# Attention loop with three score banks, maxima in a ring of three banks, and one group of projection products per unit

## The chip, the cores and the metric

The kernel runs on one core of one Trainium2 chip. The metric is the device time of one execution, in microseconds (us).

## The reference

An attention block and a sparse feed-forward, each followed by a residual add and a layer norm, in float32. x has 4 batches of 512 rows of 512 columns.

```python
q = (x @ wq).reshape(bsz, toks, NH, HD)      # 32 heads of 16
k = (x @ wk).reshape(bsz, toks, NKV, HD)     # 8 key heads
v = (x @ wv).reshape(bsz, toks, NKV, HD)
scores = jnp.einsum('bqgrd,bkgd->bgrqk', qg, k) / jnp.sqrt(jnp.asarray(HD, x.dtype))
attn = jax.nn.softmax(scores.astype(jnp.float32), axis=-1)
out = jnp.einsum('bgrqk,bkgd->bqgrd', attn, v)
return out.reshape(bsz, toks, NH * HD) @ wo
...
x = _layernorm(x + attention(x))
x = _layernorm(x + ffn(x))     # in each block of 32 of 1792 inner rows, the row with the largest mark is used
```

## The kernel before

**Tiling.** A unit is one key head of one batch with its four query heads: 4 x 8 = 32 units (NU). A unit has four key tiles of 128 keys (kt). For a unit the kernel needs the row maxima of the scores, which go into the exponent as a shift; so each score is computed twice. `scores` (L670) computes 128 query rows against 512 keys for the maxima (16 such products a unit, 48 rows of contraction: 16 dimensions in three parts, high, low and high). `row_max` (L509) reduces two banks at once on VectorE. `split_max` and `turn_max` (L689) split the maxima in two parts and transpose them, `turn_shift` (L446) on ScalarE copies them to `shift`, and a DMA (`send_shift`, L233) appends them to the queries. `scores_t` (L707) then computes the transposed scores of one key tile with 50 rows, ScalarE exponentiates them (L486), and `weigh` (L721) multiplies by v and a column of ones, so that sums and denominators come out together. ScalarE's `take_sums` (L452) takes them out of PSUM.

**Projections.** Each batch has six tasks (`project`, L645): v, four of q, and k, each 12 matmuls of 128x128 on 512 columns. ScalarE takes the high part (L440), VectorE the low part (L563), and Sync stores each to DRAM three times. V is also transposed (`turn_v`). The tasks of batches 0 to 2 stand ahead of the loop (the front), with the maxima of units 0 and 1 between them; the six of batch 3 are spread in units 0 to 2 (`LATE_AT`).

**Output projection.** After a batch is finished, its denominators are inverted (L525), spread through DRAM (`spread_reciprocals`, L257 and L259), GpSimd scales att (L412), ScalarE and GpSimd split it (`high_att` L458, L415), and TensorE does four groups of 12 matmuls (`project_out`, L737), two in each of units 5 and 6 of the next batch (`WO_AT`). VectorE adds the residual and takes the statistics (`add_tile`, L533).

**Order.** Every engine has a queue with an order written out by hand; semaphores tie them. In the loop TensorE does per key tile: transposed score 0, a maximum product, score 1, the weighted sum of the key tile before, a group if one is due, scores 2 and 3 with three maximum products, and after key tile 1 the turn of the maxima. The maxima run two units ahead, the scores of a pair that stand side by side use different halves of the array's rows.

**PSUM.** Eight banks: four for maxima (`ps_max`, two pairs), two for transposed scores (`ps_st`), one for the weighted sum (`ps_pv`), one for all else (`ps_x`).

## Time and profile before

| | us |
|---|---|
| median of 3 runs | 1004.98 (1003.74 to 1006.87) |
| the profiled execution, its own time | 998.58 |
| its span, from the first instruction to the last | 996.8 |
| front, to the first transposed score | 103.5 |
| attention loop | 486.3 |
| feed-forward | 403.9 |
| TensorE busy | 908.2 |
| VectorE busy | 562.4 |
| ScalarE busy | 442.9 |

Busy times are of one profiled execution. Matmuls are pipelined, so a busy TensorE isn't one at its peak. In the timeline a row is a run of like instructions, with its start and length; in brackets is how long the engine was idle before it and what released it. PEld is TensorE's weight load.

### The profile page before, as it was taken

To read this page: it belongs to the slowest core of one execution; us is meant where nothing else is said; L and a number is where in the kernel's file an instruction comes from. 1 tells how busy PE (TensorE), PEld (TensorE's weight loads), DVE (VectorE), ACT (ScalarE), POOL (GpSimd) and SP (SyncE) were. 2 spreads that over 40 slices of the span, in tenths; PEclk is the share of its full clock that TensorE was granted. 3 is DMA by queue.
4 is the path that set the end of the run, shared out by engine and by line. 5 is a ranking of instruction groups with operands and counts; after the bars stand their busy time and mean duration, and the time that the engine had idled before them with its cause. 6 is when DMAs were issued, how large, how long until landed. Compare 5 with 4: busy or idle time off the path is not lost. (4 is left out here: it accounts for less than half of the span.)

```text
span 996.8 us, 12134 instructions
## 1 busy us (share of the span) xinstructions
PE 908.2 (91%) x4472; PEld 533.0 (53%) x4472; DVE 562.4 (56%) x743; ACT 442.9 (44%) x821; POOL 193.1 (19%) x183
## 2 busy tenths in 40 slices
PE   5868999999899998999989975999999999999995
PEld 3745543333334333343333434777777777777774
DVE  4636567888656885468866533545563365326413
ACT  3302466777654775456765542322222222222231
POOL 6302003730210002100021002333321222122221
PEclk8889999999989998599988978999999999999998
DMA  8466535643342243323433124214030002001101
GB/s 249 160 205 240 169 110 159 175 123 91 91 117 69 76 134 80 97 85 79 135 82 109 34 97 102 82 44 155 14 116 11 1 3 103 2 1 43 42 1 42
DMA packets 50858, 92.99 MB, mean 93 GB/s; under 512 B 5648, under 2 KB 13840, under 8 KB 50288
## 3 DMA queue, kind: packets, MB, share of 16 engines
q1 hardware_dynamic: 49312, 87.05, 29.3%
q0 software_dynamic: 1488, 5.16, 1.9%
q8 instruction: 36, 0.59, 0.2%
q14 instruction: 22, 0.18, 0.1%
HBM read 56.80 MB, written 34.87 MB: 92 GB/s over the span
## 5 line engine op out<-in xcount | busy, mean ns | idle before, releaser
L509 DVE TENSOR_REDUCE neg_max<-ps_max 128x2 f32<-128x1024 f32 x256 | 302.9, 1217 | 90.1 <-PE ps_max L670 89.7
L486 ACT ACTIVATE probs<-ps_st 128x512 f32<-128x512 f32 x496 | 270.2, 595 | 142.6 <-PE ps_st L707 139.7
L707 PE MATMUL ps_st<-q,k 50*128 50x512 f32 x496 | 181.9, 511 | 28.5 <-ACT probs L486 27.6
L707 PEld LDWEIGHTS ps_st<-q,k 50*128 50x128 f32 x496 | 71.9, 192 | 203.1 <-ACT probs L486 156.8
L670 PE MATMUL ps_max<-k,q 48*128 48x512 f32 x512 | 152.8, 452 | 14.0 <-DVE neg_max L509 9.2
L721 PE MATMUL ps_pv<-probs,v 128*32 128x512 f32 x1024 | 147.3, 649 | 5.9 <-ACT probs L486 2.3
L978 POOL TENSOR_TENSOR g_l<-picked,g_h 128x512 fp32r<-128x512 f32 x56 | 73.1, 1306 | 286.9 <-ACT g_h L1017 286.9
L1003 ACT ACTIVATE mask_t<-ps_t 128x512 bf16<-128x512 bf16 x56 | 33.4, 597 | 163.6 <-PE ps_t L1199 163.6
L1211 PE MATMUL ps_h<-xt_h,w_h 128*128 128x512 f32 x224 | 93.8, 419 | 8.0 <-ACT relu L1010 8.0
L1073 DVE TENSOR_REDUCE top<-ps_prep 128x14 f32<-128x448 f32 x62 | 38.6, 623 | 99.0 <-PE ps_prep L1188 98.8
L670 PEld LDWEIGHTS ps_max<-k,q 48*128 48x128 f32 x512 | 75.6, 199 | 28.9 <-DVE neg_max L509 13.5
L1090 DVE SCALAR_TENSOR_TENSOR picked<-ps_z,relu 128x512 f32<-128x512 f32 x56 | 38.7, 691 | 90.6 <-ACT relu L1010 90.6
L1211 PE MATMUL ps_h<-xt_h,w_l 128*128 128x512 f32 x224 | 88.8, 397 | 0.0
L1211 PE MATMUL ps_h<-xt_l,w_h 128*128 128x512 f32 x224 | 88.8, 397 | 0.0
L1010 ACT ACTIVATE relu<-ps_h 128x512 f32<-128x512 f32 x56 | 33.6, 599 | 102.2 <-PE ps_h L1211 102.2
L1234 PE MATMUL ps_out<-w_h,g_h 128*128 128x512 f32 x160 | 71.2, 445 | 0.0
L1234 PE MATMUL ps_out<-w_h,g_l 128*128 128x512 f32 x160 | 63.2, 395 | 0.0
L1234 PE MATMUL ps_out<-w_l,g_h 128*128 128x512 f32 x160 | 63.0, 394 | 0.0
L1211 PEld LDWEIGHTS ps_h<-xt_h,w_h 128*128 128x128 f32 x224 | 43.1, 192 | 15.5 <-ACT relu L1010 8.1
L412 POOL TENSOR_TENSOR att<-att,inv 128x512 f32<-128x512 f32 x12 | 14.8, 1270 | 172.4 <-DMA inv<-reciprocals 172.4
L1211 PEld LDWEIGHTS ps_h<-xt_h,w_l 128*128 128x128 f32 x224 | 42.7, 191 | 9.4
L1211 PEld LDWEIGHTS ps_h<-xt_l,w_h 128*128 128x128 f32 x224 | 43.2, 193 | 6.2
(159 smaller groups left out, 1141.2 us busy)
## 6 DMA issues: line engine op xcount, KB each, us to landing
q_stacks<-parts SPq DMA_DIRECT2D x48, 256.0 KB
q<-q_stacks SPq DMA_DIRECT2D x64, 192.0 KB, 3.6
sums<-stage SPq DMA_DIRECT2D x32, 256.0 KB, 3.4
k<-k_stacks SPq DMA_DIRECT2D x64, 96.0 KB, 3.1
x_raw<-xT SPq DMA_DIRECT2D x16, 256.0 KB, 8.5
yf<-after_attention SPq DMA_DIRECT2D x4, 1024.0 KB, 5.3
w_raw<-w POOLq DMA_DIRECT2D x16, 224.0 KB, 3.1
w_raw<-w SPq DMA_DIRECT2D x14, 256.0 KB, 2.9
```

The costliest lines, as they stand in the source:

```text
L486: nc.scalar.activation(probs[kt % 2][:, r], score_bank(n, r), ACT.Exp, scale=float(HD) ** -0.5).then_inc(exp_done, 1)
L509: nc.vector.tensor_reduce(neg_max[n % 2][:, i // 2, :, i % 2], ps_max[i % 2][:], AX.X, ALU.max, negate=True).then_inc(max_red, 1)
L670: mm = nc.tensor.matmul(ps_max[i % 2][:, a], q[n % QR][64 * a:64 * a + STACK, j, t * P:(t + 1) * P], k_[n % QR][64 * a:64 * a + STACK, :], ...
L707: nc.tensor.matmul(score_bank(n, r), k_[n % QR][64 * a:64 * a + ROWS, kt * P:(kt + 1) * P], q[n % QR][64 * a:64 * a + ROWS, j, :], start=T ...
L721: last = nc.tensor.matmul(ps_pv[32 * r:32 * r + VW], v[f % 2][:, kt, g], probs[kt % 2][:, r], start=(kt == 0), stop=(kt == TT - 1))
L978: nc.gpsimd.tensor_tensor(g_l[m % 2][:], picked[m % 2][:], g_h[m % 2][:].bitcast(F32), ALU.subtract).then_inc(g_ready, 1)
L1003: nc.scalar.activation(mask_t[m % 2][:], ps_t[:], ACT.Copy).then_inc(mask_t_ready, 1)
L1010: nc.scalar.activation(act_r[m % 2][:], ps_h[:], ACT.Relu).then_inc(relu_ready, 1)
L1073: nc.vector.tensor_reduce(top[t % 2][:], src, AX.X, ALU.max).then_inc(prep_half, 1)
L1090: nc.vector.scalar_tensor_tensor(picked[m % 2][:], ps_z[:], 1.0, act_r[m % 2][:], ALU.is_equal, ALU.mult).then_inc(picked_ready, 1)
L1211: last = nc.tensor.matmul(ps_h[:], w[:, k, m * P:(m + 1) * P], xx[b % 2][:, k], start=(k == 0 and n == 0), stop=(k == KT - 1 and n == 2))
L1234: last = nc.tensor.matmul(ps_out[t][:], g[m % 2][:, t * P:(t + 1) * P], w2_tile(*w, m), start=(m == 0 and n == 0), stop=(m == MT - 1 and n ...
```

## The change

- PSUM: three banks for transposed scores (`ps_st`), three for maxima (`ps_pair`, two banks reduced by one instruction, and `ps_one`, one), one for the weighted sum, one for the rest. A maximum product waits until the bank that it writes is reduced.
- Order of a key tile on TensorE: scores 0, 1 and 2, each followed by a maximum product, then the turn of the maxima (key tile 1) or a piece of a group, then score 3 with a maximum product, and the weighted sum of the key tile before.
- Groups: only batches 0 and 1 are projected ahead of the loop, k first and v last. The six tasks of batch 2 stand in units 0 to 5, those of batch 3 in 7 to 12, the output tiles in 14 to 17, 19 to 22 and 28 to 31; one group of 12 matmuls a unit, in three pieces of four, in key tiles 2, 3 and 0 of the next (6 and 6 in the last unit).
- ScalarE takes the sums before the third exponential of key tile 0, a finished task before the second of key tile 1, and makes the shift before the third of key tile 2.
- GpSimd does the x splits of the later batches. Memory is laid out in other places. Sync loads units by the scores that are done and not by the weighted sums.

```diff
-        LATE_AT = ((0, -1), (0, 2), (1, 0), (1, 2), (2, 0), (2, 2))
-        WO_AT = ((5, 0), (5, 2), (6, 0), (6, 2))
-        HIGH_AT = ((3, 2), (3, 3), (4, 0), (4, 1))
+        TURN_V = {6: 2, 13: 3}
+        GROUPS = {}
+        for o in range(TASKS):
+            GROUPS[o] = ("task", 2, o)
+            GROUPS[7 + o] = ("task", 3, o)
+        for t in range(TT):
+            GROUPS[14 + t] = ("wo", 0, t)
+            GROUPS[19 + t] = ("wo", 1, t)
+            GROUPS[28 + t] = ("wo", 2, t)
+        HIGH_AT = {(11, r): (0, r) for r in range(REP)} | {(18, 1): (1, 0), (18, 2): (1, 1), (18, 3): (1, 2),
+                                                          (19, 0): (1, 3)} | {(27, r): (2, r) for r in range(REP)}
+        def turned_free(eng, n):
+            if n in GROUPS and GROUPS[n][0] == "task":
+                _, b, o = GROUPS[n]
+                task_taken(eng, TASKS * b + o)
+            elif n in GROUPS:
+                _, b, t = GROUPS[n]
+                eng.wait_ge(y_ready, TT * b + t + 1)
+            elif n in TURN_V:
+                eng.wait_ge(v_ready, TURN_V[n] + 1)
```

ScalarE's loop:

```diff
+                        if r == 1 and kt == 1:
+                            kind, gb, gi = GROUPS.get(n - 1, ("none", 0, 0))
+                            if kind == "task":
+                                take_task(gb, gi)
+                        if r == 2 and kt == 0 and n:
+                            take_sums(n - 1)
+                        if r == 2 and kt == 2 and n + 1 < NU:
+                            turn_shift(n + 1)
+                        if r == 3 and (n, kt) in HIGH_AT:
+                            high_att(*HIGH_AT[n, kt])
                         act.wait_ge(st_mm, i + 1)
```

VectorE's:

```diff
+                for kt in range(TT):
+                    step = n * TT + kt
+                    row_maxima(min(4 * step + 32, NT), min(4 * step + 36, NT))
+                    kind, gb, gi = GROUPS.get(n - 1, ("none", 0, 0))
+                    if kt == 0 and n + 1 < NU:
+                        split_max(n + 1)
+                    if kt == 1 and kind == "task" and gi < VTASK:
+                        low_task(gb, gi)
+                    if kt == 1 and kind == "wo":
+                        add_tile(gb, gi)
```

and TensorE's:

```diff
+                if tile >= 3:
+                    pe.wait_ge(max_red, 2 * (tile // 3) - (tile % 3 < 2))
+                dst = ps_one[:] if tile % 3 == 2 else ps_pair[:, tile % 3]
...
+            def group(n, begin, end):
+                kind, b, i = GROUPS.get(n, ("none", 0, 0))
+                if kind != "none" and begin == 0 and n + 1 < NU:
+                    pe.wait_ge(shift_ready, n + 2)
...
                 for kt in range(TT):
+                    step = n * TT + kt
+                    ahead = 4 * step + 33
                     scores_t(n, kt, 0)
+                    scores(ahead)
                     scores_t(n, kt, 1)
+                    scores(ahead + 1)
                     scores_t(n, kt, 2)
+                    scores(ahead + 2)
+                    if kt == 0:
+                        group(n - 1, 8, 12)
+                    if kt == 1 and n + 1 < NU:
+                        if n == 0:
+                            pe.wait_ge(v_ready, 2)
+                        else:
+                            pe.wait_ge(shift_ready, n + 1)
+                            turned_free(pe, n - 1)
+                        turn_max(n + 1)
+                    if kt == 2:
+                        group(n, 0, 4 if n + 1 < NU else 6)
+                    if kt == 3:
+                        group(n, 4 if n + 1 < NU else 6, 8 if n + 1 < NU else 12)
                     scores_t(n, kt, 3)
+                    scores(ahead + 3)
+                    if step:
+                        weigh(*divmod(step - 1, TT))
```

## Rows read from the trace of the kernel before

**Rows 1.** The page, busy time of each engine over the span.

```profile
PE 908.2 (91%) x4472; PEld 533.0 (53%) x4472; DVE 562.4 (56%) x743; ACT 442.9 (44%) x821; POOL 193.1 (19%) x183
```

**Rows 2.** Windows by stage: stretch, length, busy of each engine, clock, DMA, GB/s.

```profile
0.00:103.50 103.50, 75.09 (x276) 54.34 (x276) 51.60 (x63) 24.73 (x42) 28.17 (x32) 0.87 0.66 213
103.50:589.80 486.30, 450.35 (x2377) 184.50 (x2376) 330.08 (x372) 312.03 (x592) 69.15 (x75) 0.93 0.38 104
...
592.90:996.80 403.90, 382.79 (x1820) 294.19 (x1820) 180.76 (x308) 105.55 (x186) 95.75 (x76) 0.98 0.15 49
```

**Rows 3.** Waits: who for whom, total us, times, longest.

```profile
ACT probs L486 <- PE ps_st L707: 139.7, 151, 5.7
```

**Rows 4.** Timeline of one plain key tile: start, length, engine, line, instruction.

```profile
229.62 0.51 PE L707 MATMUL ps_st<-q,k 50*128 50x512 f32 x2
...
229.97 0.63 PE L670 MATMUL ps_max<-k,q 48*128 48x512 f32 x3
230.16 1.09 ACT L486 ACTIVATE probs<-ps_st 128x512 f32<-128x512 f32 x2 [0.83 <-PE ps_st L707]
230.44 2.35 DVE L509 TENSOR_REDUCE neg_max<-ps_max 128x2 f32<-128x1024 f32 x2 [0.73 <-PE ps_max L670]
...
230.90 0.46 PE L707 MATMUL ps_st<-q,k 50*128 50x512 f32 x1 [0.31 <-ACT probs L486]
...
230.91 0.49 PE L670 MATMUL ps_max<-k,q 48*128 48x512 f32 x1
...
231.30 0.49 PE L707 MATMUL ps_st<-q,k 50*128 50x512 f32 x1
...
231.72 1.07 PE L721 MATMUL ps_pv<-probs,v 128*32 128x512 f32 x8
...
232.72 0.50 PE L707 MATMUL ps_st<-q,k 50*128 50x512 f32 x2
```

**Rows 5.** Timeline of the front, ScalarE.

```profile
17.93 1.32 ACT L462 ACTIVATE w_h<-w_raw 128x512 fp32r<-128x512 f32 x2 [6.56 <-DMA w_raw<-w_qkv]
...
37.64 0.60 ACT L440 ACTIVATE parts<-ps_st 128x512 fp32r<-128x512 f32 x1 [3.41 <-DMA q_stacks<-parts]
41.49 0.60 ACT L440 ACTIVATE parts<-ps_pv 128x512 fp32r<-128x512 f32 x1 [3.25 <-DMA q_stacks<-parts]
```

**Rows 6.** Groups of instructions on VectorE: count, busy us, mean ns, idle before.

```profile
L1073 DVE TENSOR_REDUCE top<-ps_prep 128x14 f32<-128x448 f32 x62 | 38.6, 623 | 99.0 <-PE ps_prep L1188 98.8
...
L533 DVE TENSOR_TENSOR y<-ps_x,x_sb 128x512 f32<-128x512 f32 x12 | 8.3, 692 | 38.3 <-PE ps_x L737 38.3
```

**Rows 7.** Timeline, TensorE: a turn of maxima, and a group's ends.

```profile
236.85 0.60 PE L689 MATMUL ps_x<-ident,max_parts 128*8 128x128 f32 x4
237.39 0.50 PE L707 MATMUL ps_st<-q,k 50*128 50x512 f32 x1
...
301.00 0.50 PE L737 MATMUL ps_x<-wo_h,xt_h 128*128 128x512 f32 x1
...
303.95 0.50 PE L707 MATMUL ps_st<-q,k 50*128 50x512 f32 x2
```

**Rows 8.** Timeline and 5 us windows around the three stops.

```profile
268.97 0.50 PE L707 MATMUL ps_st<-q,k 50*128 50x512 f32 x1 [3.20 <-ACT probs L486]
...
275.98 0.80 PE L707 MATMUL ps_st<-q,k 50*128 50x512 f32 x2
...
281.05 0.80 PE L707 MATMUL ps_st<-q,k 50*128 50x512 f32 x2
...
390.00:395.00 5.00, 4.76 (x16) 1.64 (x16) 0.88 (x1) 2.62 (x6) 4.11 (x5) 0.50 0.00 0
515.00:520.00 5.00, 2.45 (x9) 0.48 (x9) 0.77 (x1) 2.20 (x4) 4.91 (x5) 0.56 0.14 51
```

**Rows 9.** DMA issues: count, KB each, median us to landing.

```profile
after_attention<-y SPq DMA_DIRECT2D x3, 1024.0 KB, 4.3
```

More of the change, by code:

```diff
@@ L512, in split_max, with row_maxima @@
+            def row_maxima(begin, end):
+                for tile in range(begin, end):
+                    if tile % 3 == 1:
+                        row_max(tile - 1)
+                    elif tile % 3 == 2:
+                        row_max(tile)
             def split_max(n):
-                dve.wait_ge(max_red, 8 * (n + 1))
+                at = n % 3 * TILES
+                src = neg_max[:, at:at + TILES].rearrange("p (t j a) -> p t a j", t=TT, j=2)
+                dve.wait_ge(max_red, reduces(min(TILES * (n + 1) + 2, NT)) if n + 1 < NU else reduces(NT))
@@ L631, in _, with project @@
+            variance(NB - 2)
+            norm(NB - 2)
         @block.tensor
         def _(pe):
[L633 to L647 removed]
+            def project(b, o, begin=0, end=3 * KT):
+                i = TASKS * b + o
+                j = b % 2 if b < 3 else 0
+                if begin == 0 and b < 2 and i >= 4:
+                    task_taken(pe, i - 4)
+                if begin == 0 and b == 0:
+                    pe.wait_ge(w_split, o + 1)
+                if begin == 0 and b >= 2 and o == 0:
+                    pe.wait_ge(x_low_late, KT * b)
+                for step in range(begin, end):
+                    k, n = divmod(step, 3)
+                    if n == 0 and o == 0 and b < 2:
+                        pe.wait_ge((x_low, x_low_late)[b], k + 1)
+                    last = nc.tensor.matmul(bank(i)[:], (w_h, w_l, w_h)[n][:, k, columns(o)],
+                                            (x_h, x_h, x_l)[n][j][:, k], start=(step == 0), stop=(step == 3 * KT - 1))
+                if end == 3 * KT:
+                    last.then_inc(projected, 1)
@@ L731, in project_out @@
                         pe.wait_ge(pre, 6)
-                if i:
-                    pe.wait_ge(y_ready, i)
-                pe.wait_ge(shift_ready, turns)
-                for r in range(REP):
-                    for n, (a, w) in enumerate(((att_h, wo_h), (att_h, wo_l), (att_l, wo_h))):
-                        last = nc.tensor.matmul(ps_x[:], a[:, r, t * P:(t + 1) * P], w[:, r],
-                                                start=(r == 0 and n == 0), stop=(r == REP - 1 and n == 2))
-                last.then_inc(wo_done, 1)
+                for step in range(begin, end):
+                    r, n = divmod(step, 3)
+                    a, w = ((att_h, wo_h), (att_h, wo_l), (att_l, wo_h))[n]
+                    last = nc.tensor.matmul(ps_x[:], a[:, r, t * P:(t + 1) * P], w[:, r],
+                                            start=(step == 0), stop=(step == 3 * REP - 1))
+                if end == 3 * REP:
+                    last.then_inc(wo_done, 1)
             def turn_x(t):
@@ new lines, in _ @@
+            for o in range(TASKS):
+                project(0, o)
+            project(1, 0)
+            turn_v(0)
+            project(1, 1)
+            for tile in range(0, 6):
+                scores(tile)
+            project(1, 2)
+            for tile in range(6, 12):
+                scores(tile)
+            project(1, 3)
+            for tile in range(12, 18):
+                scores(tile)
+            project(1, 4)
+            for tile in range(18, 21):
+                scores(tile)
```

620 lines of the change are left out of this document (304 added, 316 removed).

## The prediction

> **What bounds the kernel now.** I read the page's busy shares first [rows 1]: TensorE 91%, VectorE 56%, ScalarE 44%. The windows by stage then cut the span into a front (projections) of 103.5 us, the attention loop from 103.5 to 589.8, 3.1 us of storing, and the feed-forward of 403.9 us, which this change leaves alone [rows 2]. So the question is front and loop.
>
> In the loop TensorE's matmul row is busy 450 of 486 us, but its weight loads only 184.5, and the waits [rows 3] show ScalarE waiting for TensorE's scores 139.7 us, 151 times. The timeline of one key tile [rows 4] shows why. The two score products with 50 and 48 rows start together (230.90 and 230.91): they lie on different halves of the array, so a pair costs one slot. One tile is: S0 at 229.62, then M, S1 and two more M; the third exponential's score (230.90) waits 0.31 for a bank, the fourth (231.30) again; the weighted sum starts 231.72, and the next tile's score 232.72. That is 3.1 us a key tile, 12.4 a unit. Nobody is full: it is a ring of latencies. From the same rows I take: score start to exponential start 0.54; exponential start to bank free 0.74 (230.16 to 230.90); last maximum product to its reduction 0.47 (229.97 to 230.44); score to weighted sum 0.42; weighted sum to next score 1.00. Two reductions in a row take 2.35, one 1.22, so 1.13 apart.
>
> The Trainium skill (Perfetto Trace Analysis, Identifying the Most-Contended Engine) says that matmul busy time is no good measure and weight-load busy time is. The trace agrees: 93% against 38% in the loop. By the first figure there is nothing to win in the loop, by the second there would be room for a third score bank; that is the first rival below.
>
> **The front.** Each projected tile is stored three times, and the rows of ScalarE's evacuations stand 3.85 us apart (37.64, 41.49), both waiting for the store DMAs [rows 5]. The front is bound by those. It now stores 15 parts before the loop, then 10. 5 x 3.85 = 19 us go; the first task of the last batch goes too (12 matmuls, 2.95 us by the group of [rows 7]); and the maxima of the first two units, which today stand behind parts of a third batch, need only the first two. I walked the new queue: weights are in at 18 as now (17.93, same group), so part 1 is stored from 19.5 and part 4 by 35; units 0 to 2 (0.58 MB each), the next x (1 MB), v out and in (0.5 MB each) are 3.7 MB, 18 to 19 us at the 213 GB/s of the front [rows 2]; five more parts begin near 55, the one that the fourth buffer turn waits for is out near 59, the fifth is taken at 64, the first shift is sent by 69, and VectorE needs until about 73 for the remaining maxima. The loop starts at 73 instead of 103.5: -30 us. Bounds: -15 (the five stores only, partly hidden) to -38.
>
> **A plain key tile.** The new order is S0 M, S1 M, S2 M, (turn of maxima or group), S3 M, weighted sum. Three exponent banks let S3 start once exponential 0 is done: 0.5+0.74 = about 1.2 after S0 instead of being late at the fourth and fifth. But maxima have three banks instead of four, as a pair and a single, and the pair is one reduction: the product that opens the next pair waits for it. Single reductions of 512 columns do not occur; bounds are 0.62 (448 columns) and 0.69 (other 512-column reads of PSUM by VectorE) [rows 6]; I take 0.69. Four tiles a step over a ring of three gives three kinds of step. A (the fourth product opens a pair): pair complete at 0.34, reduced from 0.81 to 2.03, product at 2.1 where S3 allows 1.3; weighted sum 2.4, step 3.4. B (the third opens it): product at 1.85, then S3; step 3.4. C (the second opens it, already free): S3 at 1.2; step 2.6. Mean 3.14, so the third exponent bank is paid back to the maxima. The turn of maxima (0.53 [rows 7]) before S3 costs 0 in A, 0.4 to 0.7 in C and B, mean 0.4 a unit.
>
> Two further waits come from where things stand. The weighted sum of the last key tile of unit n-1 is now the last product of step 0 of unit n, while ScalarE takes the sums before the third exponential of that step: it sits from about 1.5 to 2.7 (C) or 3.5, then has 2 exponentials left, and S1 of the next step waits for them. It is hidden where a pair is waited for anyway and costs 1.1 elsewhere: 0.7 a unit. Plain unit: 4 x 3.14 + 0.4 + 0.7 = 13.7, with rounding 13.9, against 12.4 now.
>
> **A unit with a group.** There are 24 (12 projection tasks, 12 output tiles), in the loop now 17. Today a group costs its whole length: 301.00 to 303.95, 2.95 us [rows 7]. In pieces of four before S3 a piece takes 0.34+2x0.23+0.32 = 1.1. In A it stands in the wait (+0.1), in B and C it adds 0.8 to 1.2: 0.7 mean, 2.0 for three pieces. That would be a gain of 0.9 a group. Against it:
> - Step 1: the turn of maxima writes the bank the group used, so TensorE waits there for the take of the group. ScalarE takes it after exponential 0, VectorE only after the step's reductions, then 0.69 for its half. With S1 late from the sums, low half done at 3.4 (B), 4.2 (C), 4.3 (A) after the step's start, turn, S3, sum: step 5.6, 6.4, 6.4 instead of 3.1 to 3.9. Queued behind the wait are S3, a maximum product and the weighted sum, and for these wait ScalarE, and VectorE.
> - Step 2: the piece there waits for the shift of the next unit, which ScalarE makes after exponential 1: 2.2 at the earliest where the PE could start at 1.0. Step 4.7.
> Going through twelve steps with these durations I get 3.5+5.6+4.7+3.5 = 17.3, 4.8+6.4+4.8+4.8 = 20.8 and 3.6+6.4+4.7+3.6 = 18.3: mean 18.8 per group unit.
>
> Loop: 24 x 18.8 + 8 x 13.9 = 562, now 486.3: +76 us. Bounds: the extra waits of steps 0 to 2 all hidden, 12.5 + 2.0 a group unit and 12.5 plain = 448 (-38); and 20.8 for every group unit, 610 (+124).
>
> **Stalls that go.** Three times (near 266, 387 and 515) the loop stops for some 3.2 us, because ScalarE waits for att, scaled by GpSimd with reciprocals that come late; the first is the 3.20 before the score at 268.97. In the windows after them the granted clock is at 1.2 GHz (0.50, 0.56), and a key tile then takes 5.07 us (275.98 to 281.05) [rows 8]. The loop's mean clock of 0.93 [rows 2] is (1 - 0.93) x 2 x 486 = 68 us at 1.2 GHz. Cost now 3 x 3.2 + 68 x (1 - 3.1/5.07) = 10 + 26 = 36 us. The new places (units 11, 18, 27, the spread in 9, 17, 25) leave more units, or longer ones, between spread and need; the stops go. The 562 has none in it.
>
> **Edits at nothing.** The x splits of batches 1 to 3 move to GpSimd, which is busy 69 of 486 us in the loop [rows 2], and so does its own order there (first scaling, then the splits of w1 from unit 14 on, then the second scaling at unit 18). Without that room the second scaling would stop the loop once more, 3.2 us and a clock fall. Sync's stores of one part a unit stand behind loads that are two units early.
>
> **The tail.** The last output tile's group ends in the last unit: add and statistics (0.69 each [rows 6]), power, norm and a 1 MB store (4.3 us [rows 9]) come after it, about 8 us to the end of the stage instead of 3.1 (589.8 to 592.9 [rows 2]): +5. Bounds 0 and +8.
>
> **The clock.** New waits of TensorE in step 1 are 1.3 to 2.2 us, with thin products ahead of them. The stops of 3.2 us brought the clock down each time [rows 8]; no row says what 2 us do. I take as much loss as now, 26 us; bounds 0 and, with the clock down through all group units, 24 x 18.8 x 0.39 = 176. The Trainium skill (TensorE: Matmul & The Clock Gate, A second HAM failure mode: psum-queue depth-cycling) describes short idles between groups while PSUM banks are cycled, with the clock swinging. That speaks against this change; no run here shows such swinging yet.
>
> **Sum.** Span 996.8 - 30 + 76 + 5 + 26 = 1074; the profiled execution's own time is 1.8 above its span: 1076. The median of the runs shown is 6.4 above that execution: forecast 1082.
>
> **Rivals.**
> 1. The room is real: reductions and takes finish before TensorE reaches them, plain steps stay near 3.1, the pieces fill waits, and the stalls are gone. Loop 448 to 465, front -30, tail +5: 1005 - 30 - (38 to 21) + 5 = 942 to 959, or 975 with some of the waits. For: weight loads 38%, VectorE busy 330 of 486. Against: VectorE's single engine order puts the take behind a 1.22 reduction, by the code. It decides if a unit averages under (486+25)/32 = 16.0 us: then faster.
> 2. Waits half hidden, clock up: loop 525, 1005 - 30 + 39 + 5 = about 1020.
> 3. The clock is down in three quarters of the group units' time: 1056 (the forecast without its 26) + 131 = 1187.
> 4. The front gains nothing, as loads of units 0 to 2 now stand between the stores: forecast + 25 = 1107; within the forecast's range.
>
> **Chances.** Forecast with 4: 0.45, own range 1040 to 1130. Rival 1: 0.2. Rival 2: 0.2 (of this 0.04 near zero). Rival 3: 0.15. Eight in ten: 972 to 1165. Faster by over 0.3% (what a measurement can tell from no change): 0.2; same 0.04; slower 0.76.
>
> **What would show it.** First score of the loop near 73 us. Waits of TensorE for VectorE's maxima and, at the turn of maxima, for the take, near 40 us in sum; ScalarE's stage copy waiting for the weighted sum about 1.2 us a unit; plain units 13 to 14 us and group units 17 to 21; granted clock of the loop below 0.93. I am wrong if group units last under 16 us, or if the wait before the turn of maxima is under 0.5.

## The result, and the profile after

The changed kernel takes 1161.45 us (median of 4, 1158.01 to 1162.93) against 1004.47 of the kernel before beside it: a ratio of 1.155 [1.152, 1.159], 157 us slower. The forecast was 1082: direction right, the loss half as large. The ratios with their intervals, here and below, leave out executions over 1.5% above their kernel's fastest; the medians hold all.

The profiled execution has a span of 1161.2 us. Its page first, busy time of each engine and the granted clock in 40 slices; the first line answers to [rows 1]:

```profile
PE 993.7 (86%) x4444; PEld 547.9 (47%) x4472; DVE 571.6 (49%) x820; ACT 437.6 (38%) x813; POOL 206.8 (18%) x199
...
PEclk9677997787598789868965596979999999999999
```

Windows of its loop (stretch, length, busy of each engine, clock, DMA share, GB/s), to be held against [rows 2]:

```profile
85.80:749.80 664.00, 553.89 (x2464) 213.30 (x2462) 351.33 (x455) 314.94 (x599) 76.57 (x83) 0.79 0.29 82
```

The first transposed score is at 85.8 instead of 103.5: the front gives 17.7. The loop lasts 664.0 instead of 486.3, 177.7 more. From its end to the start of the feed-forward (757.1) it takes 7.3 instead of 3.1, and the feed-forward is as long as it was (404.1). -17.7 + 177.7 + 4.2 + 0.2 = 164.4, the difference of the spans. TensorE's busy time in the loop grew by 103.5 us. Seven tasks of 12 matmuls moved into it, about 20 us (7 times the 2.95 of [rows 7]); most of the rest is the clock, 0.79 instead of 0.93: in the best kernel below, at 0.96, the same matmuls keep TensorE busy for 431 us instead of 554. The page's clock row swings in nearly every slice from the third on, where [rows 8] had three falls.

Waits in the changed kernel (who for whom, total us, times, longest), to be held against [rows 3]:

```profile
ACT probs L569 <- PE ps_st L786: 273.7, 176, 8.3
...
ACT stage L528 <- PE ps_pv L800: 81.4, 32, 5.7
...
PE ps_pair L765 <- DVE neg_max L602: 34.3, 46, 2.6
PE ps_x L772 <- issue: 33.8, 22, 2.1
```

ScalarE waits twice as long for scores as before. The second line had hardly a counterpart in the kernel before:

```profile
ACT stage L452 <- PE ps_pv L721: 2.1, 1, 2.1
```

Now ScalarE stands in all 32 units, 2.5 us each, at the copy of the sums. The last is TensorE in front of the turn of maxima (L772), where the trace names no releaser; by the code it is the bank that ScalarE and VectorE have still to empty, and its 22 times are the units in which a group was written there. Experiment 1 bears that out.

One second key tile, of unit 9 counted from 0 (start, length, engine, line, instruction; in brackets the idle time before it and what ended it), shows these in a row:

```profile
271.50 1.07 PE L800 MATMUL ps_pv<-probs,v 128*32 128x512 f32 x8
...
272.49 0.50 PE L786 MATMUL ps_st<-q,k 50*128 50x512 f32 x1
...
272.63 0.60 ACT L528 ACTIVATE stage<-ps_pv 128x512 f32<-128x512 f32 x1 [2.03 <-PE ps_pv L800]
...
273.76 0.50 PE L786 MATMUL ps_st<-q,k 50*128 50x512 f32 x1 [0.78 <-ACT probs L569]
...
274.55 0.63 ACT L516 ACTIVATE parts<-ps_x 128x512 fp32r<-128x512 f32 x1
...
275.21 0.69 DVE L583 TENSOR_TENSOR parts<-ps_x,parts 128x512 fp32r<-128x512 f32 x1 [0.19 <-ACT parts L516]
...
276.01 1.01 PE L772 MATMUL ps_x<-ident,max_parts 128*8 128x128 f32 x4 [1.16 <-issue]
276.95 0.79 PE L786 MATMUL ps_st<-q,k 50*128 50x512 f32 x1
...
277.67 1.93 PE L800 MATMUL ps_pv<-probs,v 128*32 128x512 f32 x8
...
279.53 0.79 PE L786 MATMUL ps_st<-q,k 50*128 50x512 f32 x1
```

The sums are copied at 272.63, when the weighted sum of 271.50 is done; so the second score comes late (273.76), the take of the group at 274.55, its low half is ready at 275.90, and only then the turn of maxima starts, 3.5 us into the key tile. Across that wait the clock falls: the same score takes 0.79 after it instead of 0.50, the same weighted sum 1.93 instead of 1.07. The key tile lasts 7.04 us. The windows of 1 us around the start of the turn (the third number from the end is the clock) show the fall:

```profile
274.00:275.00 1.00, 0.84 (x4) 0.27 (x2) 0.95 (x2) 1.00 (x3) 0.00 (x0) 1.00 0.82 291
275.00:276.00 1.00, 0.00 (x0) 0.02 (x1) 0.72 (x2) 1.00 (x3) 0.00 (x0) 0.59 0.66 234
276.00:277.00 1.00, 0.99 (x6) 0.40 (x6) 0.00 (x0) 0.16 (x1) 0.00 (x0) 0.50 0.00 0
```

It is back at 2.4 GHz only in the window from 286.

**Units without a group.** Units 24 to 27 have neither a take nor a piece of a group. They were forecast at 13.9 us. Here are the first two, from one copy of the sums to the next:

```profile
592.49:613.25 20.76, 19.19 (x70) 6.35 (x70) 11.50 (x14) 9.30 (x18) 0.00 (x0) 0.50 0.34 100
613.25:633.77 20.52, 19.25 (x70) 6.27 (x70) 10.74 (x13) 9.40 (x18) 4.96 (x4) 0.50 0.43 110
```

The clock is at 1.2 GHz in both throughout, though TensorE's matmul row is busy for over nine tenths of them and never idle for more than 0.7 us. In the two after them it is 0.58 and 0.71, and they last 20.1 and 17.8 us. These four units hold 68 of the loop's 279 us at 1.2 GHz. So the low clock isn't bound to the waits of group units: once down, it stayed down where those waits are missing. In the profiled executions of seven of the kernels below the same four units had 0.77 to 0.88. What held it down here no experiment takes apart.

### The profile page after: what moved, and what is told of

Its sections match the earlier page's. It is cut to its first block and busy times, and to the rows that moved or that the text cites. A ratio compares the mean times of both kernels' runs of the same rounds, so it can differ in the third digit from the quotient of the medians.

```text
span 1161.2 us, 12454 instructions
## 1 busy us (share of the span) xinstructions
PE 993.7 (86%) x4444; PEld 547.9 (47%) x4472; DVE 571.6 (49%) x820; ACT 437.6 (38%) x813; POOL 206.8 (18%) x199
## 5 line engine op out<-in xcount | busy, mean ns | idle before, releaser
L569 ACT ACTIVATE probs<-ps_st 128x512 f32<-128x512 f32 x512 | 278.4, 601 | 274.2 <-PE ps_st L786 273.7
L602 DVE TENSOR_REDUCE neg_max<-ps_pair 128x2 f32<-128x1024 f32 x171 | 209.3, 1224 | 240.3 <-PE ps_pair L765 240.1
L786 PE MATMUL ps_st<-q,k 50*128 50x512 f32 x512 | 243.8, 548 | 32.0 <-ACT probs L569 23.3
L786 PEld LDWEIGHTS ps_st<-q,k 50*128 50x128 f32 x512 | 106.2, 228 | 246.6 <-issue 141.2
L765 PE MATMUL ps_pair<-k,q 48*128 48x512 f32 x342 | 169.2, 572 | 51.0 <-DVE neg_max L602 34.3
L800 PE MATMUL ps_pv<-probs,v 128*32 128x512 f32 x1024 | 179.4, 782 | 0.0
L605 DVE TENSOR_REDUCE neg_max<-ps_one 128x1 f32<-128x512 f32 x170 | 116.5, 685 | 50.0 <-PE ps_one L765 49.4
L765 PEld LDWEIGHTS ps_pair<-k,q 48*128 48x128 f32 x342 | 67.1, 225 | 80.2 <-DVE neg_max L602 56.6
L765 PE MATMUL ps_one<-k,q 48*128 48x512 f32 x170 | 93.9, 552 | 1.5 <-DVE neg_max L605 1.2
L772 PE MATMUL ps_x<-ident,max_parts 128*8 128x128 f32 x128 | 24.2, 323 | 33.8 <-issue 33.8
L1317 PEld LDWEIGHTS ps_h<-xt_h,w_h 128*128 128x128 f32 x224 | 43.5, 194 | 15.2 <-ACT relu L1116 7.8
```

What stands on the lines that cost most here:

```text
L569: nc.scalar.activation(probs[kt % 2][:, r], ps_st[i % 3][:], ACT.Exp, scale=float(HD) ** -0.5).then_inc(exp_done, 1)
L602: nc.vector.tensor_reduce(neg_max[:, at:at + 2], ps_pair[:], AX.X, ALU.max, negate=True).then_inc(max_red, 1)
L605: nc.vector.tensor_reduce(neg_max[:, at:at + 1], ps_one[:], AX.X, ALU.max, negate=True).then_inc(max_red, 1)
L765: nc.tensor.matmul(dst, q[n % QR][64 * a:64 * a + STACK, j, t * P:(t + 1) * P], k_[n % QR][64 * a:64 * a + STACK, :], start=True, stop=Tru ...
L786: nc.tensor.matmul(ps_st[i % 3][:], k_[n % QR][64 * a:64 * a + ROWS, kt * P:(kt + 1) * P], q[n % QR][64 * a:64 * a + ROWS, j, :], start=Tr ...
L800: last = nc.tensor.matmul(ps_pv[32 * r:32 * r + VW], v[f % 2][:, kt, g], probs[kt % 2][:, r], start=(kt == 0), stop=(kt == TT - 1))
```

## What a microsecond at 1.2 GHz costs

To separate waits from clock a price is needed. One kernel of the experiments (shift early, below) had four executions of different length: spans 1117.0, 1121.9, 1140.8 and 1161.4 us at a mean clock of 0.896, 0.888, 0.869 and 0.846. The time at 1.2 GHz is 2 x (1 - clock) x span: 232 us in the first, 358 in the last. 44.4 us of span for 125 us: 0.35 each (the forecast had 0.39, from one key tile of [rows 8]). Only one of the four has a trace, so that they differ in nothing but the clock isn't shown. Four executions each of the kernels with the early take, the three moves and the early weighted sum, fitted by a line, give 0.36, 0.36 and 0.34; whole groups and the kernel before with att later, which vary as much in clock, give 0.29 and 0.27, and the others scatter from 0.1 to 0.5. Units 24 to 27 give another reading: 79.1 us at a clock of 0.57 in the changed kernel, 71.6 at 0.82 in the one with dummy matmuls, which has none in them, and 5.9 of these are a stop for a shift: 13.4 us for 42, or 0.32. I take 0.35 and give for each kernel the loop of its profiled execution, its clock, the clock's cost (0.35 x 2 x (1 - clock) x loop) and what is left, the loop's length at full clock. It is an estimate; the medians stand beside it, since the profiled execution stands up to 30 us off them by its clock. With 0.29 the changed kernel would have 81 for the clock and 583 left, the kernel before 20 and 467. The experiments were measured at four times, with the kernel before beside them at medians of 1004.1 to 1009.5; so differences of some 5 us between experiments say nothing.

| kernel | median us | ratio [95%] | loop | clock | its cost | left |
|---|---|---|---|---|---|---|
| before | 1004 | | 486.3 | 0.93 | 24 | 462 |
| changed | 1161 | 1.155 [1.152, 1.159] | 664.0 | 0.79 | 98 | 566 |
| take early | 1132 | 1.115 [1.103, 1.128] | 637.1 | 0.84 | 71 | 566 |
| shift early | 1133 | 1.112 [1.103, 1.120] | 663.3 | 0.78 | 102 | 561 |
| sums late | 1102 | 1.091 [1.082, 1.101] | 600.4 | 0.88 | 50 | 550 |
| weighted sum early | 1081 | 1.071 [1.065, 1.077] | 598.8 | 0.86 | 59 | 540 |
| single reductions | 1130 | 1.121 [1.114, 1.128] | 647.0 | 0.76 | 109 | 538 |
| dummy matmuls | 1117 | 1.109 [1.102, 1.117] | 619.5 | 0.92 | 35 | 585 |
| whole groups | 1150 | 1.137 [1.127, 1.147] | 661.6 | 0.81 | 88 | 574 |
| three moves | 1042 | 1.033 [1.022, 1.044] | 541.6 | 0.91 | 34 | 508 |
| two moves + weighted sum early | 1065 | 1.054 [1.046, 1.062] | 570.5 | 0.88 | 48 | 523 |
| three moves + singles | 986 | 0.976 [0.971, 0.982] | 483.0 | 0.94 | 20 | 463 |
| the same + shift sent first | 962 | 0.956 [0.952, 0.961] | 458.6 | 0.96 | 13 | 446 |
| the same, x later | 962 | 0.956 [0.950, 0.961] | 463.3 | 0.95 | 16 | 447 |
| shift sent first, with whole groups | 985 | 0.977 [0.971, 0.983] | 490.0 | 0.93 | 24 | 466 |
| kernel before, att four key tiles later | 978 | 0.973 [0.964, 0.981] | 472.6 | 0.96 | 13 | 459 |

By this the loop rose by 104 us in waits and moved groups, and by 74 in clock. The hand count of the forecast had 562 at full clock; 566 is left.

## Experiments

Theory W: the price is made by waits, of ScalarE for the sums, of TensorE for the take and for the shift, and the clock that goes with them. Theory M: the ring of three maxima with its pair reduction sets the pace, whatever else is late.

**1. Take early.** ScalarE and VectorE take the group a key tile before the turn of maxima.

```diff
-                        if r == 1 and kt == 1:
+                        if r == 3 and kt == 0:
                             kind, gb, gi = GROUPS.get(n - 1, ("none", 0, 0))
...
-                    if kt == 1 and kind == "task" and gi < VTASK:
+                    if kt == 0 and kind == "task" and gi < VTASK:
                         low_task(gb, gi)
-                    if kt == 1 and kind == "wo":
+                    if kt == 0 and kind == "wo":
                         add_tile(gb, gi)
```

> Theory W (waits made by where the takes stand, and the clock that falls in them): the finished group is taken by ScalarE before the fourth exponential of key tile 0 and by VectorE after the reductions of key tile 0, so the turn of maxima no longer waits for it. A group unit loses about 2.0 us, 24 x 2.0 = 48 us, and of the 279 us at 1.2 GHz about half go, 0.39 x 140 = 55 us more: 1161 - 103 = 1058 us, loop near 560. Rival M (the ring of three maximum banks sets the pace and the clock falls with it whatever the takes do): at most 20 us, 1140 or more, loop clock still 0.79.

1131.9 us, 30 less, and what is left at full clock didn't move. ScalarE's wait for the sums stayed at 82.4. TensorE's wait ahead of the turn (33.8 us) is gone, but its waits for maxima grew from 28.5 to 41.5, for exponentials from 23.3 to 29.0 and for the shift's transfer from 8.6 to 16.7. So the late take alone isn't the limit; most of its wait went over to the others. W had it too large.

**2. All three moves.** Take early, the sums ahead of the first exponential of key tile 1, the shift ahead of the fourth exponential of key tile 1.

```diff
-                        if r == 2 and kt == 0 and n:
+                        if r == 0 and kt == 1 and n:
                             take_sums(n - 1)
...
-                        if r == 2 and kt == 2 and n + 1 < NU:
+                        if r == 3 and kt == 1 and n + 1 < NU:
                             turn_shift(n + 1)
```

> As before this one, and also the sums are taken after the four exponentials of key tile 0 and the shift is made before the fourth exponential of key tile 1. W: group units 15.6, plain units 13.2, loop 24 x 15.6 + 8 x 13.2 = 480, with 20 us for the clock 500: 86 + 500 + 8 + 404 + 2 = 1000 us, loop clock 0.93 or more. M: over 1100 us.

1042.2: 119 less. Between the profiled executions it is 123, of which 59 are in what is left and 64 in the clock. The wait for the sums is 18.8 us instead of 81.4. W is mostly right, M is not the whole; but 40 us over its number, so something of M is in it.

**3. Dummy matmuls for the clock.** The changed kernel with eight 128x128x512 matmuls into the bank of the fourth score ahead of the wait for the take, in 22 units. They compute nothing that is used.

```diff
                             pe.wait_ge(shift_ready, n + 1)
+                            if n - 1 in GROUPS:
+                                i3 = step * REP + 3
+                                pe.wait_ge(exp_done, i3 - 2)
+                                pe.wait_ge(pre, 6)
+                                for d in range(8):
+                                    nc.tensor.matmul(ps_st[i3 % 3][:], wo_h[:, d % REP, 0:P], wo_h[:, d % REP],
+                                                     start=True, stop=True)
                             turned_free(pe, n - 1)
```

> The changed kernel with eight more matmuls of 128x128 on 512 columns in key tile 1 of each of 23 group units, written to the score bank that the fourth score overwrites, ahead of the wait for the take; 1.8 us at 2.4 GHz in a wait of 1.3 to 2.6 us. They do no work. If the clock is the mis-sized term (109 us): the clock stays at 2.4 GHz for most of the loop, loop 560 to 590, 1161 - 85 = 1076 us. If the waits alone are the cost: 1161 or up to 20 us more.

1116.8. Its loop:

```profile
84.60:704.10 619.50, 522.69 (x2640) 223.43 (x2638) 352.74 (x455) 315.01 (x599) 76.79 (x83) 0.92 0.32 88
```

With TensorE kept busy through that one wait the clock goes from 0.79 to 0.92, 279 us at 1.2 GHz to 99. 180 x 0.35 = 63 us come back; 44.5 are seen, the rest would be the dummies' own time (176 x 0.23 = 40 us of work, about 18 of it then on the path; it is what the price leaves over, not a measurement). That is 40 us short of the 1076 expected. So with matmuls in the wait of step 1 most of the clock is kept, and a higher clock gives time. Not all of it is gained in the units that have the dummies: units 24 to 27, which have none, went from 0.57 to 0.82, 42 of the 180 us. That this one wait brought the clock down doesn't follow either: experiment 1 took the same wait away without adding matmuls, other waits grew in its place, and the clock came back only to 0.84.

**4. The kernel before, one stage later.** Where ScalarE waits for att, its copies are put four key tiles later; nothing of the change is in it.

```diff
-        HIGH_AT = ((3, 2), (3, 3), (4, 0), (4, 1))
+        HIGH_AT = ((4, 0), (4, 1), (4, 2), (4, 3))
```

> The kernel before, with the four splits of att on ScalarE at key tiles 0 to 3 of unit 4 of a batch instead of (3,2), (3,3), (4,0), (4,1). W: the three stops and the clock falls behind them go, 10 + 26 us: 1004.5 - 36 = 968 us, loop clock 1.00. Rival: the stops go but the clock falls for another reason: 994 us.

977.8 us. TensorE's longest wait for exponentials in the loop is 0.5 us, where it was 3.3: the stops are gone. The clock is 0.96 and not the expected 1.00. The stops' price of 36 us in the forecast was about right (31 against the kernel before beside it): what the change could gain there, one line gains without it.

**5. Weighted sum early.** Half of the change undone: the weighted sum goes back behind the second score.

```diff
                     scores(ahead + 1)
+                    if step:
+                        weigh(*divmod(step - 1, TT))
                     scores_t(n, kt, 2)
...
                     scores(ahead + 3)
-                    if step:
-                        weigh(*divmod(step - 1, TT))
```

> The changed kernel with one half of the change undone: the weighted sum of the key tile before stands after the second score again instead of at the end of the key tile; everything else stays. With this the last weighted sum of a unit is done before ScalarE reaches the third exponential, where it takes the sums. Theory W (the loss is made by waits in steps 0 to 2 of a unit, each adding its own length): ScalarE's wait of 81 us for the weighted sum goes to under 20, and with half of the step's rest hidden and the clock that comes back, the loop shortens by 35 to 45 us: 1120. Theory O (the waits overlap: VectorE and ScalarE are late at the turn of maxima whatever the sums do): under 10 us, 1152 or more. Theory M (the ring of three maxima sets the pace): the same, under 10 us, with TensorE's waits for the maxima grown by what the sums no longer cost.

1080.5: 81 less, the largest effect of one edit, twice W's number. ScalarE's wait for the sums went from 81.4 to 22.6, and TensorE's waits for the shift (15.0 us ahead of the pieces in the changed kernel) are gone too.

**6. Shift early** alone (the second edit of experiment 2).

> The changed kernel with ScalarE's copy of the next unit's shift put ahead of the fourth exponential of the second key tile, instead of after the second exponential of the third, where TensorE's group pieces wait for it. Theory W: 24 group units gain 0.8 to 1.2 us each in step 2, 19 to 29 us, and some clock: 1130. Theory O (overlap with the other late things): under 10 us, 1152 or more.

1133.1 (1118.7 to 1163.1), 28 less as W said, and nearly all of it clock: what is left moved by 5. The 15.0 us of TensorE ahead of the pieces are gone; 8.3 came back as wait for the shift's transfer.

**7. Singles.** The three moves, and VectorE reduces each tile of maxima by itself.

```diff
-                dve.wait_ge(max_mm, tile + (2 if tile % 3 == 0 else 1))
+                dve.wait_ge(max_mm, tile + 1)
...
-                if tile % 3 == 0:
-                    nc.vector.tensor_reduce(neg_max[:, at:at + 2], ps_pair[:], AX.X, ALU.max,
-                                            negate=True).then_inc(max_red, 1)
-                else:
-                    nc.vector.tensor_reduce(neg_max[:, at:at + 1], ps_one[:], AX.X, ALU.max,
-                                            negate=True).then_inc(max_red, 1)
+                src = ps_one[:] if tile % 3 == 2 else ps_pair[:, tile % 3]
+                nc.vector.tensor_reduce(neg_max[:, at:at + 1], src, AX.X, ALU.max, negate=True).then_inc(max_red, 1)
...
-                    pe.wait_ge(max_red, 2 * (tile // 3) - (tile % 3 < 2))
+                    pe.wait_ge(max_red, tile - 2)
```

> The kernel with the three moves (take of the group, shift and sums where nothing waits for them; 1042 us measured), in which VectorE now reduces every tile of maxima singly as soon as its product is there, instead of the pair in one instruction of 1.22 us. Theory M (prediction's key tile types A and B: the pair's reduction holds the product that opens the next pair, step 3.4): steps go from a mean of 3.14 to VectorE's own pace of 4 x 0.685 = 2.74 and a little, say 2.85, 0.3 us in 128 steps, 37 us, with TensorE's waits for the maxima under half of now: 1005. Theory P (the plain step is paced by the score, exponential, bank ring and the maxima wait in its shadow): 1042 within 8.

986.0, 56 less, and below the kernel before. VectorE works more (4 x 0.683 in place of 2.55 us a key tile on the mean) and the kernel is faster: what fits is how long a bank is held. Its groups of reductions:

```profile
L602 DVE TENSOR_REDUCE neg_max<-ps_pair 128x1 f32<-128x512 f32 x321 | 211.1, 683 | 68.1 <-PE ps_pair L758 64.8
L602 DVE TENSOR_REDUCE neg_max<-ps_one 128x1 f32<-128x512 f32 x160 | 109.3, 683 | 32.9 <-PE ps_one L758 31.7
```

TensorE's waits for the maxima in the loop fell from 43.4 + 3.9 us (three moves) to 9.3 + 4.1. Its largest wait is now another:

```profile
PE ps_st L779 <- DMA q<-shift: 29.8, 4, 11.6
```

**8. Two moves with the weighted sum early.** Take and shift early, the sums where the change takes them, the weighted sum behind the second score.

> The weighted sum after the second score again, with the take of the group and the shift moved early as in the kernel with the three moves, and ScalarE's taking of the sums left where the change has it. If only ScalarE's wait for the sums was the price of the weighted sum's place, this is the three moves kernel by another way: 1042 within 10. If the place itself costs (the sum at the end stands between the fourth score and the next tile's first, so the first exponential of every key tile comes later), it is faster by 15 us or more.

1065.2, 23 slower than the three moves: neither guess had that. The second, that the place at the end costs by itself, is out. Behind the second score TensorE waits 12.4 us for exponentials ahead of the weighted sum, a wait that the three moves don't have. The two kernels differ in the take of the sums as well, so that the end is the better place isn't shown by itself.

**9. Singles alone**, on the changed kernel.

> The changed kernel with nothing moved, but with every tile of maxima reduced singly by VectorE (0.685 us) as soon as its product is there, instead of the pair in one instruction of 1.22. On top of the three moves this took 56 us. Theory M (the pair's reduction is a term of its own, in every key tile): the same 50 to 60 us here, about 1105, and more if the shorter reductions also bring VectorE to the take of the group sooner, 1090. Theory O (here the waits of step 1 stand over it, and it shows only once they are gone): under 20 us, 1140 or more.

1129.5: 32 less, between the two theories. At full clock 28 go, but its clock is lower still (0.76); TensorE's waits for the maxima fall from 28.5 to 4.1 us, about as much as goes, while ScalarE's wait for the sums (65.3) and the late take (31.6) are still there.

**10. Shift sent first.** As 7; Sync sends the shift ahead of the spread of reciprocals.

```diff
-                if b and g == 1 and b < NB:
-                    spread_reciprocals(b - 1)
                 if n + 1 < NU:
                     send_shift(n + 1)
+                if b and g == 1 and b < NB:
+                    spread_reciprocals(b - 1)
```

> The three moves and the single reductions (986 us measured), and Sync now sends the next unit's shift ahead of the spread of reciprocals, whose second transfer waits for the first. In the 986 us kernel TensorE stood three times, 11.6, 6.5 and 8.0 us, at a unit's first transposed score for that shift. If nothing stands behind it the 26 us go, and with them some of the clock that is lost in the windows after (37 us at 1.2 GHz more or less by 0.36 each): 950 to 960. Rival: the wait moves to the attention tile two units on, since the spread now starts later: 980.

962.2 (957.7 to 965.2): 24 less, the rival is out. Of the three stops one is left, of 3.2 us. This is the best kernel, 0.956 [0.952, 0.961] of the one before. Its loop:

```profile
85.20:543.80 458.60, 431.15 (x2463) 180.55 (x2462) 352.99 (x615) 315.82 (x599) 77.09 (x83) 0.96 0.42 119
```

**11. Sums late** alone (the first edit of experiment 2).

> The changed kernel with one move alone: ScalarE takes the sums of unit n-1 ahead of the first exponential of the second key tile of unit n instead of ahead of the third exponential of the first. It ends ScalarE's wait for the weighted sum, as the weighted sum after the second score did (81 us less), but leaves that sum at the end of the key tile. If the wait for the sums was what that kernel won: the same, 1080 within 15. If the sum's place at the end of the key tile costs by itself beside the pair reductions: 1110 or more.

1101.5, 60 less: neither number. It ends the same wait of ScalarE (19.6 us remain) as experiment 5 did with 81. The intervals of the two don't meet, so the 21 between them are real. By TensorE's waits, experiment 5 has 8.8 us less ahead of the turn and none of the 17.0 for the shift, but 11.5 more for exponentials ahead of the weighted sum; the rest stays open.

**12. x later.** As 10, with the third batch's x loaded behind three part stores of batch 1 instead of ahead of all.

```diff
             load_unit(0)
-            for k in range(KT):
-                load_x(2, k)
             load_unit(1)
...
                 store_part(1, o)
+                if o == 2:
+                    for k in range(KT):
+                        load_x(2, k)
```

> As the kernel with moves, single reductions and the shift sent first, with the load of the third batch's x (1 MB) put behind three of the five part stores of batch 1 instead of ahead of them. In the front 16 DMA engines carry some 205 to 213 GB/s. If the front is bound by what they carry ahead of the last stores: 1 MB less is 4.9 us, first transposed score at 79 instead of 84. If it is bound by the chain of the last part's store, the unit loads and the turn of maxima: 83 to 85. The loop must not lose: the first group needs this x split at about 6 us into the loop.

962.0, and the first transposed score at 87.0 instead of 85.2: 1 MB less ahead of the first three stores, up to 4.9 us by the expectation, brings nothing, so the front isn't bound by what the DMA engines carry there.

**13 and 14. Whole groups.** The other half of the change undone, on the changed kernel and on that of experiment 10.

```diff
-                    if kt == 0:
-                        group(n - 1, 8, 12)
...
                     if kt == 2:
-                        group(n, 0, 4 if n + 1 < NU else 6)
+                        group(n, 0, 12)
...
-                    if kt == 3:
-                        group(n, 4 if n + 1 < NU else 6, 8 if n + 1 < NU else 12)
```

> The changed kernel with the other half of the change undone: the twelve matmuls of a group stand in one piece ahead of the fourth score of the third key tile, instead of in three pieces of four in three key tiles; nothing else is moved. Theory W (prediction: a piece costs 0.7 us on the mean since part of it stands in a wait, 2.1 a group; a whole group costs its length of 2.95, less the one wait it stands in): 0.5 to 0.9 us more for each of 24 groups at full clock, +12 to +20 us, 1180. But it also ends a key tile earlier, so VectorE and ScalarE can take it a key tile before the turn of maxima needs the bank, in step 1: theory C (what costs is TensorE waiting among thin products and the clock that goes with it, and a dense group of 3 us feeds the clock): 1100 or less. Rival: the place of the pieces doesn't matter, 1160 within 10.

> The same undoing in the kernel with the three moves, single reductions and the shift sent first (962 us), where the take is early already and the clock is near full (0.96 in the loop). Here the pieces' own price shows: theory W: they hide in waits that a whole group can't use, so the whole group costs 0.5 to 0.9 us more each, +12 to +20, 978. Rival: the plain steps are by now paced by VectorE's 2.74 us of single reductions and a whole group stalls it once instead of thrice: 962 within 6, or faster.

1150.2 on the changed kernel, 11 less, about what its clock accounts for (0.81): near the guess that the place doesn't matter, and far from the 1100 of theory C. 985.4 on the best, 23 more. The pieces are worth 1 us a group, as the forecast said (0.9), but only where nothing else is late. In the changed kernel they give nothing. The loss came from the late things, not from the pieces.

## Why the forecast was right in sign and half the size

**The step that failed: "I take as much loss as now, 26 us", the clock.** It cost 98 by the price above (81 with 0.29). This term was short by 72 of the 87 us between the forecast's span (1074) and the measured one; 12 are the front, 4 the loop's count. The prediction had named the place (waits of 1.3 to 2.2 us in step 1, with thin products ahead), had the bounds 0 and 176, and took a value near the low one because only stops of 3.2 us had brought the clock down in [rows 8]. The rows above and below show falls after waits of 0.8 and 1.2 us and of 0.8 and 2.1 us in one key tile, and experiment 3 that matmuls in one of them give most of the clock back. It also had tied the low clock to the group units, in its bound as in the third rival; a quarter of the time at 1.2 GHz lay in the four units without a group. The third rival (clock down through three quarters of the group units' time, 1187) was nearer in its mechanism than the forecast; with 98 for its 131 it would have said 1154.

The Trainium skill (TensorE: Matmul & The Clock Gate, A second HAM failure mode: psum-queue depth-cycling) tells of short idles between groups that make the clock swing; the trace agrees, with 0.79 in the loop and falls in most of its slices. It puts the loss into the price of going up and down; here units 24 and 25, in which the clock doesn't change, are among the slow ones, and the time at 1.2 GHz itself is the price.

**The loop's own count** held, within what the price leaves open: 562 forecast, 566 left at full clock (583 with 0.29), of which 7 are a stop that the count didn't have. By unit it held as well: five runs of group units (1 to 5, 8 to 12, 15 to 17, 20 to 22, 29 and 30) lasted 20.9, 23.7 (with the stop), 20.1, 21.0 and 22.0 us a unit at clocks of 0.87, 0.74, 0.92, 0.84 and 0.73; less the clock's cost that is 19.0, 19.4, 19.0, 18.6 and 17.8 for the forecast's 18.8. Units 24 to 27, 19.8 each, come to 13.8 for its 13.9. The single reduction was taken at 0.69 and measured 685 ns, the pair at 1.22 and measured 1224. In step 1 the low half was to be done 3.4 us after the step's start in type B, 4.2 or 4.3 in C and A. In the key tile shown (the third product opens the pair: B) it is 275.90 - 272.49 = 3.4. In one where the pair is complete only with the second product (A) it is 134.21 - 129.94 = 4.3:

```profile
129.94 0.50 PE L786 MATMUL ps_st<-q,k 50*128 50x512 f32 x1
...
131.22 0.50 PE L786 MATMUL ps_st<-q,k 50*128 50x512 f32 x1 [0.78 <-ACT probs L569]
...
133.53 0.68 DVE L583 TENSOR_TENSOR parts<-ps_x,parts 128x512 fp32r<-128x512 f32 x1
...
134.31 0.60 PE L772 MATMUL ps_x<-ident,max_parts 128*8 128x128 f32 x4 [2.11 <-issue]
...
135.26 1.94 PE L800 MATMUL ps_pv<-probs,v 128*32 128x512 f32 x8
...
137.13 0.79 PE L786 MATMUL ps_st<-q,k 50*128 50x512 f32 x1
```

The steps were then longer than counted (7.04 and 7.2 for 5.6 and 6.4) by the clock that fell there. That these parts were in the loop is confirmed by taking them out: three moves take 59 at full clock, singles on top 45. Two sizes were off: ScalarE's wait for the sums was put at 1.2 us a unit and is 2.5, and TensorE's for maxima and take at 40 us and is 62; the count came out in spite of it, which is in part luck.

**The front** was to give 30 and gave 17.7. The walk let the parts of batch 1 follow their stores and had the fifth taken at 64; it was taken at 74.67. The trace (TensorE, then ScalarE's takes of the parts) has the last three 8.2 to 9.4 apart:

```profile
48.41 0.80 PE L765 MATMUL ps_pair<-k,q 48*128 48x512 f32 x2 [16.61 <-DMA q<-q_stacks]
...
51.88 0.79 PE L740 MATMUL ps_st<-x_h,w_h 128*128 128x512 f32 x1
...
57.05 0.50 PE L765 MATMUL ps_pair<-k,q 48*128 48x512 f32 x2
...
59.67 0.50 PE L765 MATMUL ps_pair<-k,q 48*128 48x512 f32 x2 [1.88 <-DVE neg_max L602]
...
60.98 0.79 PE L740 MATMUL ps_st<-x_h,w_h 128*128 128x512 f32 x1
```

```profile
57.16 0.60 ACT L516 ACTIVATE parts<-ps_st 128x512 fp32r<-128x512 f32 x1 [17.22 <-PE ps_st L740]
66.51 0.60 ACT L516 ACTIVATE parts<-ps_st 128x512 fp32r<-128x512 f32 x1 [8.75 <-PE ps_st L740]
74.67 0.60 ACT L516 ACTIVATE parts<-ps_st 128x512 fp32r<-128x512 f32 x1 [7.56 <-PE ps_st L740]
```

TensorE first stands 16.6 us until unit 0 is loaded (4.6 in the kernel before). Then a part is 12 matmuls, 5.2 us at 1.2 GHz (51.88 to 57.05) where [rows 7] has 2.95 at the full clock, and then six maxima products, 3.9 us (57.05 to 60.98), held by a pair reduction. The front is bound by TensorE's order there; experiment 12 shows that it isn't the 1 MB of x.

**The stops that go**: the three waits for att are gone (no row of ScalarE for GpSimd's att is left, where it was 7.9 us in 3), but one stop came in their place, and the forecast had none. Ahead of unit 10 TensorE stands 7 us:

```profile
283.35 0.64 SPq L297 DMA_DIRECT2D inv<-reciprocals  x1
...
284.04 1.35 SPq L268 DMA_DIRECT2D q<-shift  x2
...
296.61 0.79 PE L786 MATMUL ps_st<-q,k 50*128 50x512 f32 x1 [6.95 <-DMA q<-shift]
```

The shift was ready at 281.90 and is sent at 284.04, behind the spread (Sync waits between its two transfers) and behind its 1 MB; TensorE can start at 296.61. The forecast's sentence on Sync, whose stores "stand behind loads that are two units early", was about one part of Sync's queue, and the spread, which stands behind the send in the kernel before and ahead of it in the changed one, was not walked. In the slow changed kernel it showed once; in the faster one of experiment 7 three times, 26 us, and experiment 10 took all but 3 us of them away.

**The tail** was put at +5 and is +4.2. The fourth rival's +25 is a slip: a front that gains nothing is 30 more than the forecast.

**What the wrong rivals had.** "The room is real" needed units under 16 us. The best kernel has them (458.6 / 32 = 14.3, with the same three banks and the same pieces), at 962 against the 942 to 975 of that rival. So the room was there: a unit of the kernel before takes 15.2 with its stops, and the best kernel wins less than 1 us a unit on it, though with seven more groups in the loop, when take, sums, shift, reductions and the send all come in time. The Trainium skill (Perfetto Trace Analysis, Identifying the Most-Contended Engine) would judge TensorE's headroom by weight loads: 32% in the changed loop (213.30 of 664), 39% in the best. The trace shows that the headroom wasn't used up in either; what moved the time were waits between the engines, and the clock.

**Open**: how the clock's loss divides among the three waits of a group unit, and what keeps the clock down in units 24 to 26. Executions of one kernel differ by up to 44 us in it, so the single edits (experiments 1, 6, 9, 13) rank the waits poorly.

## What to carry to other kernels

When the order of one engine is changed, go through every instruction that another engine has at a fixed place in its own order (a take, a copy of sums, a send in the DMA queue) and ask what it stands behind at its new hour: here three lines of ScalarE's order, two of VectorE's, one of Sync's and the width of a reduction made 1161 into 962. In this ring of three banks the shorter hold of a bank was worth more than fewer instructions. And short waits that repeat in a dense loop are to be counted twice, once for their length and once for TensorE's clock; of bounds 0 and 176 the clock took 98 here, so if several stand in one key tile, neither bound is the one to forecast from, and units without such waits belong in it too.

## What the runs showed of the hardware

- After two waits of TensorE in a key tile (0.8 and 1.2 us, 0.8 and 2.1 us) the granted clock fell from 2.4 to 1.2 GHz; the loop's mean fell to 0.79, and to 0.76 where the maxima were quicker.
- The clock stayed at 1.2 GHz through two whole units (592.5 to 633.8) in which TensorE's row was busy 38.4 of 41.3 us and never idle for more than 0.7 us.
- A microsecond at 1.2 GHz cost about 0.35 us in this loop, in which TensorE partly waits (0.27 to 0.36 over the kernels whose clock varied most).
- VectorE's maximum over 512 columns of PSUM takes 0.685 us, over 1024 columns in one instruction 1.224: the pair saves 0.15 us and holds two banks.
- One program's executions differed by 4% (1118.7 to 1163.1 us), in step with the clock (0.896 to 0.846).
